# Edge features and times multiplied by their weight matrix per edge, ahead of the scatter, so that the table of edges holds rows of 132 floats

## The chip, the cores and the metric

The kernel runs on one core of one Trainium2 chip. The metric is the time of one execution on the device, in microseconds; it takes 11116.84 us (median of 3 runs, 11109.44 to 11128.29).

## The reference

A graph of N = 12,500 nodes with 64 features and E = 200,000 edges (`src`, `dst`) goes through two networks, with a layer normalisation after each. The first network has three layers that gather the neighbours' rows and sum them per source node; its weights are 64x64. The second network, which the change is about, also uses three arrays of 200,000 x 64 floats, the edge features `ef`, the source times `stf` and the edge times `et`:

```python
target_vec = concat([node_feature[node_j], ef, et], axis=1)      # N_edges x 192
neighbor_emb = target_vec @ W1.T + b1                             # 192 -> 64
neighbors_sum = relu(segment_sum(neighbor_emb, node_i, N))
source_node_vec = segment_sum(concat([node_feature[node_i], stf]), node_i, N) / max(cnt, 1)
out = concat([neighbors_sum, source_node_vec], axis=1) @ W2.T + b2
```

Each edge counts in both directions, and each node has one edge to itself (no features, times of the first edge). The product with W1 is linear, so it can be taken per edge or after the sum over a node's edges.

## The kernel before, in words

All matrix work is in tiles of 128 nodes (T = 98 tiles). Edges are put in order by pairs of tiles: K = 4 places for edges make a chunk, 128 chunks a block, and there are NB = 544 blocks. The stages, in order:

1. **Clear and rank.** SyncE clears the table `by_src` in DRAM, (544 + 1) x 512 rows of ROW floats, by 34 transfers and a few small ones (lines 403 to 408). Beside it a histogram of tile pairs is counted. Then comes ranking, 313 steps of 5 columns of 128 edges: VectorE makes one-hots and masks (`rank`, line 1299), TensorE adds them up and looks the running counts up, five "lanes" per step (`rank`, line 708: three matmul calls per lane, lines 716, 719 and 721), ScalarE copies the running counts out of PSUM before every lane (`snap`, line 972), and VectorE picks out the place of each edge (`select`, line 1290), which goes to `pos`.
2. **Moves.** 2 x 68 `moves` work out which chunk goes where for the gathers: VectorE compares (line 1329), TensorE multiplies with one moving column (line 736, 8 products, 16 passes).
3. **Scatter, beside 1 and 2 and beyond.** SyncE loads batches of PB = 11 columns of edges into one of three slots of `prow`: `ef`, `et`, `stf` (line 418), the three numbers of `meta` (line 419) and the places `ppos` (line 422). GpSimd writes each column to the table by one indirect DMA of 128 rows (line 580, 1562 of them, and one short one at line 593), after the clear is done. SyncE waits on `s_pout` (line 414) before it fills a slot again. VectorE waits for the last scatter at line 1354 and then makes the node array.
4. **wide_by_dst.** Per block, 544 times: GpSimd gathers 128 chunks of 4 rows of the table (line 613); TensorE transposes one-hots (line 747), sums the features by tile with fp32 matmuls (`feature_sum`, line 759: 4 products, 8 passes, the moving operand has FEAT = 193 columns) and picks node rows (line 752); VectorE adds FEAT columns to `node` (line 1414); `rows` has 8 slots.
5. **wide_by_src, then three layers of the first network,** each with a spread (DRAM bound writes of `gathered`) and a sums stage (`sums`, line 825): groups of 4 blocks, in each GpSimd's 4 gathers (line 650), 16 bf16 matmuls (line 836), VectorE's reduction, one-hots and adds, and beside them one block of the features summed by source: SyncE fetches a block of the table to `frows` (2 slots, line 517), TensorE runs `feature_sum` on it, and VectorE adds FEAT columns (line 1479). There are four such stages.
6. **The last layer** (`last`, lines 870 and 1605) takes the sums `facc` of features, times and count and multiplies by W1 and W2.

Every engine runs its own list in order; semaphores order them. Nothing is planned by a program.

## Time and profile before

| | us |
|---|---|
| median of 3 runs | 11116.84 |
| profiled execution, its own time | 11130.16 |
| span of its trace | 11128.4 |
| TensorE busy | 6864.9 (62%) |
| VectorE busy | 6383.6 (57%) |
| GpSimd busy | 5207.2 (47%) |
| ScalarE busy | 3581.3 (32%) |
| moved by DMA | 2320.61 MB, mean 209 GB/s |

The profiled execution is 13 us above the median. A share of busy time is an average over stages that have different limits; the stages are told apart by their windows in the rows below. The granted TensorE clock is printed from 0 to 1, where 1.0 is 2.4 GHz and 0.5 is 1.2 GHz. In a windows row the start and end and the length are followed by busy time and (count) of TensorE's matmuls (PE), its weight loads (PEld), VectorE (DVE), ScalarE (ACT) and GpSimd (POOL), then the granted clock, the DMA share and GB/s. SP is SyncE; a q behind an engine's name is its sequencer.

### The profile page before, as it was taken

Reading aid. Unit: us, or ns where it says so; the run is one execution under the profiler, and the core shown is the slowest. Engines: PE = TensorE matmul, PEld = TensorE weight load, DVE = VectorE, ACT = ScalarE, POOL = GpSimd, SP = SyncE. Lnnn points to the kernel's source line nnn. Section 1 sums busy time; section 2 is a strip of 40 time slices with the busy share of each in tenths; the row PEclk is TensorE's granted clock in tenths of the full one; section 3 lists DMA queues with packets and bytes.
Section 4 is the critical chain, followed back from the end, with each engine's and each line's share of the span. In section 5 each row is a group of like instructions: output and inputs, shape, how many; then the busy total and the mean of one; then the engine's idle time right before and its main releaser. Section 6 shows DMA issues by size and latency. Waiting matters only on the chain.

```text
span 11128.4 us, 191621 instructions
## 1 busy us (share of the span) xinstructions
PE 6864.9 (62%) x46640; PEld 6050.2 (54%) x46640; DVE 6383.6 (57%) x15194; ACT 3581.3 (32%) x10119; POOL 5207.2 (47%) x4833
## 2 busy tenths in 40 slices
PE   7899977800039999556465664556635566656665
PEld 6688867800028888444345554455534455445555
DVE  8899972300036666444575555755567555665556
ACT  0233320000027777333392113921129411481111
POOL 0068887866644444666005661056610366206650
PEclk9999999999999999777697776977769887897776
DMA  9965555555569989556396663966629766896670
GB/s 384 388 179 144 144 144 124 123 142 139 139 176 304 302 297 294 164 166 162 91 396 216 192 188 100 393 220 191 188 51 354 270 191 192 262 361 194 192 172 12
DMA packets 1567388, 2320.61 MB, mean 209 GB/s; under 512 B 974516, under 2 KB 1046056, under 8 KB 1567320
## 3 DMA queue, kind: packets, MB, share of 16 engines
q1 hardware_dynamic: 1227608, 1356.73, 36.5%
q0 software_dynamic: 292608, 911.36, 29.7%
q10 hardware_dynamic: 47104, 51.75, 1.9%
q8 instruction: 26, 0.43, 0.0%
q14 instruction: 42, 0.34, 0.0%
HBM read 1328.55 MB, written 986.78 MB: 208 GB/s over the span
## 4 chain that ended last, share of the span: by engine, by line
issue 28%; PE 22%; DVE 19%; another core or an unknown queue 9%; DMA 9%; ACT 7%; DVEq 5%; ACTq 1%; POOL 1%; SPq 0%; POOLq 0%
PE ps L759 8%; DMA gathered<-ring 5%; PE ps L736 4%; DVE mask L1309 3%; PE ps L836 3%; ACT ring L1074 2%; DVEq L371 2%; ACT hring L1084 2%; PE ps L752 2%; DVE node L1500 2%; DMA frows<-by_src 2%; DVE ohj L1227 1%; DVE oh_s L1368 1%; DVE prod L1293 1%
## 5 line engine op out<-in xcount | busy, mean ns | idle before, releaser
L650 POOL DMA_INDIRECT ring<-gathered,gidx x2176 | 2170.3, 997 | 3328.7 <-DMA gathered<-ring 2118.5
L580 POOL DMA_INDIRECT by_src<-prow,ppos x1562 | 1958.2, 1254 | 1228.5 <-DMA ppos<-pos 707.2
L1382 DVE TENSOR_REDUCE red<-ps 128x256 f32<-128x768 f32 x680 | 650.0, 956 | 1645.5 <-remote 1227.7
L1462 DVE CAST ring<-ps 128x384 bf16<-128x384 f32 x2176 | 1087.5, 552 | 367.7 <-PE ps L752 346.6
L752 PE MATMUL ps<-hring,oht_g 128*128 128x192 bf16 x8704 | 872.4, 246 | 614.9 <-DVE ring L1462 204.7
L836 PE MATMUL ps<-ring,oht_g 128*128 128x192 bf16 x8704 | 1075.5, 286 | 174.7 <-issue 117.5
L759 PE MATMUL ps<-frows,oh_s 128*128 128x193 f32 x2176 | 658.4, 470 | 837.2 <-issue 565.5
L1074 ACT CAST ring<-ps 128x384 bf16<-128x384 f32 x2176 | 1124.5, 519 | 10.6 <-PE ps L752 10.4
L836 PEld LDWEIGHTS ps<-ring,oht_g 128*128 128x128 bf16 x8704 | 954.7, 127 | 291.3 <-issue 251.6
L752 PEld LDWEIGHTS ps<-hring,oht_g 128*128 128x128 fp8e4 x8704 | 659.0, 97 | 828.3 <-issue 786.1
L719 PE MATMUL ps<-snap,oht_e 98*128 98x98 f32 x3130 | 1056.4, 441 | 0.0
L759 PEld LDWEIGHTS ps<-frows,oh_s 128*128 128x128 f32 x2176 | 547.4, 278 | 887.8 <-issue 860.0
L1084 ACT COPY hring<-node 128x192 bf16 x2176 | 853.0, 393 | 55.3 <-issue 46.2
L759 PE MATMUL ps<-rows,ohf 128*128 128x193 f32 x4352 | 848.7, 338 | 26.1 <-ACT ohf L999 19.9
L747 PE MATMUL ps<-ident_bf,oh 128*128 128x128 bf16 x2176 | 211.2, 220 | 1054.2 <-DVE oh L1368 1054.1
L613 POOL DMA_INDIRECT rows<-by_src,gidx x544 | 518.9, 954 | 728.9 <-PE ps L759 265.8
L719 PEld LDWEIGHTS ps<-snap,oht_e 98*128 98x128 f32 x3130 | 819.9, 322 | 0.0
L972 ACT COPY snap<-ps 98x98 f32<-98x98 f32 x1565 | 379.4, 242 | 1182.8 <-PE ps L716 748.5
L747 PEld LDWEIGHTS ps<-ident_bf,oh 128*128 128x128 bf16 x2176 | 167.7, 114 | 1054.8 <-issue 1054.5
L759 PE MATMUL ps<-frows,hring 128*128 128x193 f32 x2176 | 514.9, 390 | 361.0 <-issue 255.1
L759 PEld LDWEIGHTS ps<-rows,ohf 128*128 128x128 f32 x4352 | 700.1, 191 | 43.6 <-ACT ohf L999 30.9
L634 POOL DMA_INDIRECT ring<-gathered,gidx x544 | 558.1, 1026 | 331.2 <-issue 153.4
(226 smaller groups left out, 12892.2 us busy)
## 6 DMA issues: line engine op xcount, KB each, us to landing
gathered<-ring SPq DMA_DIRECT2D x544, 768.0 KB
by_src<-zeros SPq DMA_DIRECT2D x34, 6272.0 KB, 46.3
frows<-by_src SPq DMA_DIRECT2D x544, 392.0 KB
oht_g<-oht SPq DMA_DIRECT2D x544, 256.0 KB, 6.2
gathered<-got SPq DMA_DIRECT2D x136, 776.0 KB
prow<-in_edge_attr_n SPq DMA_DIRECT2D x284, 352.0 KB
bc<-tidrow ACTq DMA_DIRECT2D x313, 160.0 KB
prow<-in_edge_attr SPq DMA_DIRECT2D x142, 352.0 KB
```

The source lines that it names most:

```text
L580: pool.indirect_dma_start(out=table, out_offset=bass.IndirectOffsetOnAxis(ap=ppos[:, s, j:j + 1], axis=0), in_=prow[:, s, j, :], in_offset ...
L613: pool.indirect_dma_start(out=rows[:, c % 8, :, :].rearrange("p k w -> p (k w)"), out_offset=None, in_=table_chunks, in_offset=offsets(g, ...
L634: pool.indirect_dma_start(out=ring1[:, c, :], out_offset=None, in_=gb1, in_offset=offsets(g, c % 4)).then_inc(q.got[g], 16)
L650: pool.indirect_dma_start(out=ring[:, c, :], out_offset=None, in_=gb, in_offset=offsets(g, c % 4)).then_inc(q.got[g], 16)
L719: pe.matmul(where, oht_e[0:T, v, l * P:(l + 1) * P], snap[0:T, (u * LANES + l) % 2, :], start=True, stop=False, skip_group_check=True).the ...
L752: mm = pe.matmul(ps[:, bank + k // 2, k % 2 * HW:(k % 2 + 1) * HW], eight(one_hots)[:, k * P:(k + 1) * P], parts, start=True, stop=True, s ...
L759: mm = pe.matmul(ps[:, bank, 0:FEAT], one_hots[:, k, :], rows_of[:, k, 0:FEAT], start=k == 0, stop=k == K - 1)
L836: mm = pe.matmul(ps[:, 2 * u + e // 2, e % 2 * 256:e % 2 * 256 + HW], ohq[:, c % 8, :, k], ring[:, c, k * HW:(k + 1) * HW], start=k == 0, ...
L1074: act.copy(ring[:, c, 0:2 * HW], ps[:, 2 * (c % 4), 0:2 * HW]).then_inc(q.g, 1)
L1084: act.copy(hring[:, e, :], parts_at(at[e])).then_inc(q.hc, 1)
L1382: return dve.tensor_reduce(red[:, u, :, 0:D], four_of(bank)[:, :, 0:HW].rearrange("p e (a d) -> p e d a", d=D), AX.X, ALU.add)
L1462: dve.tensor_copy(ring[:, c, 2 * HW:4 * HW], ps[:, 2 * (c % 4) + 1, 0:2 * HW]).then_inc(q.gv, 1)
```

## The change

The edge features and edge times of each column (128 edges x 128 floats) are transposed on TensorE and multiplied there by the two matching parts of W1 (`w_z`, 128 x 64), and the product z (64 floats per edge) takes the place of both in the row to be scattered. A row is then z, `stf`, and four small numbers: ROW goes from 196 to 132 floats, FEAT from 193 to 129. The table, its clear, the gathers of stage 4 and the fetches of `frows` shrink with it.

A unit is three columns: 3 transposes (`raw_turned`), one ScalarE copy out of PSUM (`raw_kept`, 128 x 384 fp32), 3 fp32 products with 64 columns (`z_product`), one ScalarE copy into `prow` (`z_kept`, 128 x 192). There are 521 units: 312 stand in the rank steps, one in each (the transposes behind lane 0, the products of the unit before behind lane 2, the ScalarE copies at lanes 2 and 4), 204 in the moves, 6 beside every 4 moves, and 5 behind them. A batch is now 6 columns (two units); a batch's row needs five transfers as before (two into `praw`, three into `prow` and `ppos`). `z_kept` waits until the slot's scatter is done; the scatter waits for `s_z` as well. TensorE waits for all the weights before ranking, and for `s_z` and `s_sel` between ranking and moves. In the last layer the identity stands in the matrix for z, and the self edge's times take the place of the feature sums.

```diff
-PB = 11
-PBATCHES = COLS // PB
-EF, ET, STF, ONE, LS, LD, ROW = 0, D, 2 * D, 3 * D, 3 * D + 1, 3 * D + 2, 3 * D + 4
+ZF, STF, ONE, LS, LD, ROW = 0, D, 2 * D, 2 * D + 1, 2 * D + 2, 2 * D + 4
 FEAT = ONE + 1
+PB = 6
+UC = 3
+UNITS_R = STEPS // 6 * 6
+UNITS_M = 6
...
+PTURNS = (UNITS_R + 2 * (NG // 4) * UNITS_M) // 6
+UNITS = 6 * PTURNS + 5
...
+            def raw(s, use, cols, first=False):
+                if not first:
+                    sp.wait_ge(s_rawt, 6 * use + (2 * s - 4))
+                    sp.nop(nofuse=True)
+                for f, c in ((ef, 0), (et, D)):
+                    v = f[0:P * COLS].rearrange("(c p) d -> p c d", p=P)
+                    sp.dma_start(praw[:, s, 0:cols, c:c + D], v[:, bass.ds((3 * use + s) * PB, cols), :]).then_inc(s_raw[s], 16)
+            def row(s, use, cols, first=False):
                 if not first:
                     sp.wait_ge(s_pout[s], use * (PB * 16))
-                sp.nop(nofuse=True)
-                cols = bass.ds((3 * use + s) * PB, PB)
-                for f, c in ((ef, EF), (et, ET), (stf, STF)):
-                    v = f[0:P * COLS].rearrange("(c p) d -> p c d", p=P)
-                    sp.dma_start(prow[:, s, :, c:c + D], v[:, cols, :]).then_inc(s_plod[s], 16)
-                sp.dma_start(prow[:, s, :, ONE:ROW], meta[:, cols, :]).then_inc(s_plod[s], 16)
-            def places(s, use):
-                sp.dma_start(ppos[:, s, :], pos[:, bass.ds((3 * use + s) * PB, PB)]).then_inc(s_plod[s], 16)
-            AHEAD = -(-3 * PB // LANES)
-            sp.wait_ge(s_meta, 1)
+                    sp.nop(nofuse=True)
+                at = bass.ds((3 * use + s) * PB, cols)
+                v = stf[0:P * COLS].rearrange("(c p) d -> p c d", p=P)
+                sp.dma_start(prow[:, s, 0:cols, STF:STF + D], v[:, at, :]).then_inc(s_plod[s], 16)
+                sp.dma_start(prow[:, s, 0:cols, ONE:ROW], meta[:, at, :]).then_inc(s_plod[s], 16)
+                sp.dma_start(ppos[:, s, 0:cols], pos[:, at]).then_inc(s_plod[s], 16)
...
+            RANKED = STEPS // 4
+            sp.wait_ge(s_tids, 2)
             for s in range(3):
-                load(s, 0, True)
-            sp.wait_ge(s_pos, AHEAD)
+                raw(s, 0, PB, True)
+            sp.wait_ge(s_pos, 4)
             for s in range(3):
-                places(s, 0)
-            with sp.Fori(1, STEPS // AHEAD) as i:
+                row(s, 0, PB, True)
+                raw(s, 1, PB)
+            with sp.Fori(1, RANKED) as i:
                 for s in range(3):
-                    load(s, i)
                     if s == 0:
-                        sp.wait_ge(s_pos, i * AHEAD + AHEAD)
+                        sp.wait_ge(s_pos, 4 * i + 4)
                         sp.nop(nofuse=True)
-                    places(s, i)
+                    row(s, i, PB)
+                    raw(s, i + 1, PB)
...
-                pool.wait_ge(s_plod[s], use * 80 + 80)
+                pool.wait_ge(s_plod[s], use * 48 + 48)
+                pool.wait_ge(s_z, 6 * use + (2 * s + 2))
...
+            def raw_turned(n, v, bank, s, use, first=False):
+                u, h = v % 2, v % 2
+                pe.wait_ge(s_raw[s], 32 * use + 32)
+                if not first:
+                    pe.wait_ge(s_rawc, n - 1)
+                for j in range(UC):
+                    mm = pe.transpose(ps[:, bank + u, j * P:(j + 1) * P], praw[:, s, UC * h + j, :], ident[:, :])
+                mm.then_inc(s_rawt, 1)
+            def z_product(n, v, bank, first=False):
+                u = v % 2
+                pe.wait_ge(s_rawc, n + 1)
+                if not first:
+                    pe.wait_ge(s_z, n - 1)
+                for j in range(UC):
+                    mm = pe.matmul(ps[:, bank + 2 + u, j * D:(j + 1) * D], rawT[:, u, j * P:(j + 1) * P], w_z[:, :],
+                                   start=True, stop=True)
+                mm.then_inc(s_zmm, 1)
...
+                    if l == LANES - 1:
+                        mm.then_inc(s_t, 1)
+                    if l == 0 and m is not None:
+                        raw_turned(n, u, 4, u // 2, m, begin and u < 2)
+                    if l == 2 and not (begin and u == 0):
+                        z_product(n - 1, u + 5, 4, begin and u < 3)
...
+            pe.wait_ge(s_z, UNITS_R)
+            pe.wait_ge(s_sel, STEPS)
...
+                def turn(m, first):
+                    use = UNITS_R // 6 + (k - 1) * (NG // 4)
+                    for v in range(6):
+                        n = 6 * m + (6 * use + v)
+                        if v in (0, 2, 3, 5):
+                            moves(4 * m + (0, 0, 1, 2, 0, 3)[v], (0, 0, 1, 0, 0, 1)[v])
+                        raw_turned(n, v, 0, v // 2, m + use)
+                        if not first or v > 0:
+                            z_product(n - 1, v + 5, 0)
...
+            act.dma_start(w_z[:, :], W1t[D:3 * D, :]).then_inc(s_wload, 16)
+            act.dma_start(w_n1[0:D, :], W1t[0:D, :]).then_inc(s_wload, 16)
+            act.dma_start(w_n1[D:P, :], W1t[2 * D:3 * D, :]).then_inc(s_wload, 16)
...
+            def raw_kept(n, v, bank, first=False):
+                u = v % 2
+                act.wait_ge(s_rawt, n + 1)
+                if not first:
+                    act.wait_ge(s_zmm, n - 1)
+                act.copy(rawT[:, u, :], ps[:, bank + u, 0:UC * P]).then_inc(s_rawc, 1)
+            def z_kept(n, v, bank, s, use, first=False):
+                u, h = v % 2, v % 2
+                act.wait_ge(s_zmm, n + 1)
+                if not first and h == 0:
+                    act.wait_ge(s_pout[s], use * (PB * 16))
+                act.copy(prow[:, s, UC * h:UC * h + UC, ZF:ZF + D],
+                         ps[:, bank + 2 + u, 0:UC * D].rearrange("p (c d) -> p c d", d=D)).then_inc(s_z, 1)
...
+                    if l == 2 and m is not None:
+                        raw_kept(n, u, 4, turn == 0 and u < 2)
+                    if l == 4 and u > 0:
+                        z_kept(n - 1, u - 1, 4, (u - 1) // 2, m, turn == 0)
+                    elif l == 4 and turn > 0:
+                        z_kept(n - 1, 5, 4, 2, UNITS_R // 6 - 1 if m is None else m - 1, turn == 1)
...
+            dve.tensor_copy(w_n2[0:D, 0:D], ident[0:D, 0:D])
...
-                    dve.tensor_scalar(cat[:, :, D:P], facc[:, ts, EF:EF + D], 1.0, None, ALU.mult).then_inc(q.cat, 1)
+                    dve.tensor_copy(cat[:, :, D:P], unit_t).then_inc(q.cat, 1)
...
-                    dve.tensor_tensor(cat2[:, :, 0:D], facc[:, ts, ET:ET + D], unit_t, ALU.add)
+                    dve.tensor_scalar(cat2[:, :, 0:D], facc[:, ts, ZF:ZF + D], 1.0, None, ALU.mult)
```

## Rows read from the trace of the kernel before

**Rows 1.** Windows by stage: stretch, length, busy us (instructions) per engine, clock, DMA, GB/s.

```profile
14.00:630.00 616.00, 514.53 (x2939) 424.73 (x2937) 537.19 (x1367) 81.54 (x332) 0.00 (x0) 1.00 1.00 379
630.00:1610.00 980.00, 929.59 (x4973) 801.92 (x4972) 940.03 (x2469) 299.12 (x1234) 823.16 (x502) 1.00 0.58 143
1610.00:2195.00 585.00, 458.11 (x2144) 457.70 (x2144) 167.94 (x141) 0.00 (x0) 459.65 (x359) 1.00 0.50 123
2195.00:3190.00 995.00, 0.00 (x0) 0.00 (x0) 0.00 (x0) 0.00 (x0) 676.28 (x703) 1.00 0.56 140
3270.00:4450.00 1180.00, 1078.68 (x8541) 999.81 (x8539) 734.43 (x2670) 873.08 (x2263) 502.39 (x528) 1.00 0.92 299
5883.00:6712.00 829.00, 509.93 (x3136) 465.88 (x3136) 463.10 (x1040) 98.82 (x263) 530.53 (x536) 0.77 0.68 188
7276.00:8120.00 844.00, 511.92 (x3184) 466.96 (x3184) 471.23 (x1054) 100.39 (x265) 537.56 (x543) 0.78 0.67 188
8739.00:9590.00 851.00, 513.95 (x3184) 467.49 (x3185) 471.34 (x1055) 100.39 (x265) 553.87 (x544) 0.78 0.68 188
9975.00:10850.00 875.00, 535.02 (x3271) 488.03 (x3271) 486.66 (x1095) 102.66 (x269) 537.84 (x544) 0.77 0.68 185
```

**Rows 2.** The clears: their issue (first and last start), size and landing; first scatter.

```profile
L408 SPq DMA_DIRECT2D by_src<-zeros x34: 782/16608/24364, 14.4 to 561.4; - x34
...
by_src<-zeros SPq DMA_DIRECT2D x34, 6272.0 KB, 46.3
...
634.07 1.14 POOL L580 DMA_INDIRECT by_src<-prow,ppos  x1 [632.53 <-DMA ppos<-pos]
```

**Rows 3.** Groups of instructions in ranking, 640 to 1600 us: busy us, mean ns.

```profile
L719 PE MATMUL ps<-snap,oht_e 98*128 98x98 f32 x2448 | 826.1, 441 | 0.0
L580 POOL DMA_INDIRECT by_src<-prow,ppos x490 | 811.7, 1656 | 149.4 <-issue 149.4
```

**Rows 4.** Groups of instructions in the moves, 1745 to 2195 us.

```profile
L736 PE MATMUL ps<-steps,cmp 99*128 x2080 | 443.9, 352 | 3.2 <-DVE cmp L1329 3.2
...
L580 POOL DMA_INDIRECT by_src<-prow,ppos x266 | 368.6, 1386 | 91.3 <-issue 80.8 <-DMA ppos<-pos 10.5
```

**Rows 5.** One rank step in order of time, VectorE and GpSimd: start, us, instruction.

```profile
999.97 0.96 POOL L580 DMA_INDIRECT by_src<-prow,ppos  x1 [0.30 <-issue]
...
1000.14 0.45 DVE L1227 TENSOR_TENSOR ohi<-tid_s,bin_lane 128x490 bf16<-128x490 bf16 x1
...
1001.24 2.32 POOL L580 DMA_INDIRECT by_src<-prow,ppos  x1 [0.30 <-issue]
...
1001.33 1.40 DVE L1309 SCALAR_TENSOR_TENSOR mask<-bc,tid_f,upper_bf 128x128 bf16<-128x128 bf16 x5
...
1002.64 0.70 DVE L1293 TENSOR_TENSOR prod<-ps,ohj 128x490 f32<-128x490 f32 x1
```

**Rows 6.** fp32 transposes and products of a layer, in order of time.

```profile
5397.03 1.75 PE L853 MATMUL ps<-ident,ring 128*128 128x128 f32 x7 [8.14 <-DVE ring L1558]
5398.58 3.19 PE L859 MATMUL ps<-wts,ring 128*128 128x128 f32 x14
```

**Rows 7.** Feature matmuls in wide_by_dst, 3300 to 4450 us: busy us, mean ns.

```profile
L759 PE MATMUL ps<-rows,ohf 128*128 128x193 f32 x4156 | 808.7, 338 | 21.4 <-ACT ohf L999 16.5 <-issue 4.4
```

**Rows 8.** SyncE's register moves, 1745 to 2195 us and 2200 to 3150 us (min/median/max ns).

```profile
L418 SPq MOVE prow<-in_edge_attr_n x50: 5/29/29, 1745.0 to 2194.9; - x50
...
L418 SPq MOVE prow<-in_edge_attr_n x120: 1/698/1421, 2208.4 to 3140.3; - x120
```

**Rows 9.** Chain that ended last, by line: wide_by_dst, first and last sums stage.

```profile
by line: PE ps L759 40.6%; PE ps L752 10.1%; issue 8.8%; another core or an unknown queue 8.4%; ACT ohf L999 8.0%; PE ps L747 7.6%; ACT got L1006 6.6%; DMA rows<-by_src,gidx 4.5%; ACT loc L1016 1.8%; ACT loc L993 1.3%; DVE got L1396 0.3%; A
...
by line: issue 33.1%; another core or an unknown queue 15.5%; PE ps L759 11.4%; PE ps L836 10.1%; DVEq L371 5.6%; DVE node L1500 5.1%; DVE oh_s L1368 4.6%; DVE red L1382 3.9%; DMA frows<-by_src 2.8%; DVEq L1500 2.1%; DVE node L1479 1.7%; DV
...
by line: issue 30.5%; another core or an unknown queue 16.2%; PE ps L759 9.0%; PE ps L836 7.3%; DVEq L371 6.0%; DMA frows<-by_src 5.6%; DVE node L1500 5.3%; DVE red L1382 5.0%; DVE oh_s L1368 4.8%; DVEq L1500 2.8%; DVE node L1479 1.6%; DVE 
```

**Rows 10.** Size of the fetches of the table in the sums stages.

```profile
frows<-by_src SPq DMA_DIRECT2D x544, 392.0 KB
```

135 lines of the change are left out of this document (81 added, 54 removed).

## The prediction

> **What bounds the kernel now.** I read the windows by stage first. Clear, ranking, moves and scatter take the first 3190 us; then come wide_by_dst (3270 to 4450) and four sums stages of 829 to 875 us, 3399 us together [rows 1]. In the first 3190 us the last thing to end is the scatter: it starts at 634 us, because its semaphore of the clears comes last (34 transfers of 6272 KB, the last one issued at 561.4 and landing some 46 us later, near 608), and GpSimd then issues 1563 indirect DMAs [rows 2]. From 14 to 630 us the DMA share is 1.00, so the clear is bandwidth. Behind it GpSimd sets the time, at three paces: 490 scatters in 960 us of ranking, 1.96 us each [rows 3]; 266 in 450 us of moves, 1.69 us [rows 4]; 703 in the last 995 us, 1.42 us, in which TensorE, VectorE and ScalarE do nothing [rows 1].
>
> Why three paces: a scatter takes 0.96 us and the next starts 0.30 later, 1.27 us in all, unless it starts while VectorE runs the run from the first one-hot to the last mask (1000.14 to 1002.64, 2.5 us). The one that started at 1001.24 took 2.32 us and ended 0.9 us after that run; the one at 999.97 took 0.96 [rows 5]. So a step of T us has room for 1 + floor((T - 2.5) / 1.27) scatters: 2 at the present 3.92 us (960 us over 2448/10 steps), as the 490 in 960 us show, and 3 from 5.04 us on. In the moves each of the 130 compares costs a scatter (450 - 10.5 - 266 x 1.27) / 130 = 0.79 us [rows 4].
>
> **The clear.** ROW goes to 132/196 = 0.673 of its size, so the 594 us of clears become 400 us and end near 414 instead of 608. But ranking now waits for the first `praw`, which is queued on SyncE behind the clears, and cannot start before they have landed: I put it at 418; now it starts near 1600 - 313 x 3.92 = 373. Four steps and the loads of a batch later the scatter starts, near 450, 184 us earlier than now.
>
> **Ranking.** TensorE is busy 929.59 us in 980 [rows 1], 3.7 us per step. A unit adds three fp32 transposes and six fp32 passes. Seven transposes take 1.55 us before the products start, 0.22 each [rows 6]; a pass with a single moving column takes 443.9 / 2080 = 0.213 us in the moves [rows 4], so 64 columns cost about that too. Unit: 3 x 0.22 + 6 x 0.213 = 1.94 us. The bounds of one transpose or pass are 0.13 us (808.7 / 4156 = 0.195 for 193 columns, scaled to 128 [rows 7]) and 0.34 us (826.1 / 2448, the look-ups [rows 3]): 1.2 to 3.0 us per unit. I take 1.94, since the moves stand right behind ranking. A step then lasts 5.65 us, bound by TensorE: VectorE needs 3.92, and GpSimd needs 5.04 for the three columns that a step now supplies. 313 steps are 1768 us, ending near 2186 (now: 1600). ScalarE's two copies fit into its idle time (299 us busy of 980); the one that waits for `s_pout` stands ahead of the next `snap`, and behind that all of ranking would wait, but with GpSimd at 5.04 against 5.65 it seldom does.
>
> **Moves.** 34 turns of 18 columns. TensorE: 6 x 1.94 + 4 x 3.42 (16 passes) = 25.3 us. GpSimd: 18 x 1.27 + 4 x 0.79 = 26.0 us. With both so near each other I take 27 us: 918 us. I add 20 us for the lag of the scatter behind the units, 17 for the last 15 columns' own path and 20 for a slow start of the moves. The scatter ends near 3161, against 3190: 29 us gained, of the 184 that the clear gives. The rest goes because the last 995 us at 1.42 us a column are replaced by ranking at 5.65/3 = 1.88. Should a unit cost 1.2 us, GpSimd's 5.04 is the step and ranking is 190 us shorter; at 3.0 us it is 330 us longer. These are the ends for this part: gain 220, loss 300.
>
> SyncE issues five transfers per batch as before, but a batch is 6 columns. In the moves its register instructions take 29 ns, and in the idle tail 698 ns [rows 8]; a batch of 11 columns then took 995 x 11 / 703 = 15.6 us. I cost it at nothing, since TensorE and VectorE now work until the end of the scatter; what it costs without that cover is the second rival.
>
> **wide_by_dst.** Its chain goes for 40.6% of 1150 us, 467 us, through the feature matmuls, and for 4.5% through the gathers of the table [rows 9]. Both shrink by a third with FEAT and ROW: 156 + 17. Against that, ScalarE is busy 873 of 1180 us and VectorE 734 [rows 1] with waits on registers besides, so something of it is taken over: I take 140, bounds 40 and 230 (the DMA share of 0.92 falls as well, which may free more).
>
> **Sums stages.** The feature matmuls hold 11.4% of the chain in the first and 9.0% in the last, the `frows` fetches 2.8% and 5.6% [rows 9]: 347 and 143 us over the 3399. The fetch goes from 392 KB [rows 10] to 264. A third of both is 163 us. GpSimd's floor is 544 x 1.27 = 691 us per stage, below the 829 to 875, so it does not stop this; VectorE's own order and its tile reads do in part. I take 110, bounds 0 and 200. The node array is narrower too (its memset ahead of wide_by_dst): 5 us. The last layer exchanges operations one for one: nothing.
>
> **Sum.** 29 + 5 + 140 + 110 = 284 us off the profiled execution's 11130 us (span 11128.4 plus 1.8): 10,846. The median of the runs is 13 us lower, so 10,830 us.
>
> **Rivals.**
> (1) Ranking is bound by GpSimd, not TensorE: a step of about 5.1 us. For it: the feature matmuls do 193 columns in 0.195 us, so a pass with 64 might be short [rows 7]; against it: the 0.213 us passes right beside. It gives 313 x 0.55 = 172 us more: 10,660 us. The Trainium skill ("TensorE: Matmul & The Clock Gate", section "LDWEIGHTS (loading the stationary operand)") says that a weight load takes its columns divided by 1.2 in ns, 107 ns for 128; by that nine loads make a unit of 0.96 us, an estimate from the page, and this rival would hold. The moves' passes, with 128 loaded columns and one moving one, take twice that, so the trace disagrees there.
> (2) Slower: SyncE ticks at 0.70 us an instruction during the moves. Its price: 3 batches x 15.6 = 46.7 us a turn instead of 27, 670 us if it holds for all 34 turns: 11,500 us. It decides from 284 / 19.7 = 14 turns on. For it: ticks are there in the whole idle tail, and batches are smaller; against it: none in the moves now [rows 8].
> (3) Ranking steps of 6.6 us, because ScalarE's waits and the hand-overs between units add up on TensorE: 313 x 0.95 = 297 us more: 11,125 us, no change.
> (4) The set-up as forecast, but wide_by_dst and sums hardly shrink, since the matmuls' wait was beside VectorE's: 50 us in all instead of 250: 11,030 us.
>
> **How the numbers follow.** Forecast 0.50, (1) 0.12, (2) 0.12, (3) 0.12, (4) 0.14. What can be told from no change is 0.2%, 22 us. Faster: 0.50 + 0.12 + 0.14 and half of (3), 0.82; same 0.03; slower: (2) and the rest of (3), 0.15. The forecast's own range is 10,700 to 10,980 (set-up +-110, the stages +-90). To hold eight in ten I reach to most of (1) and to (3): 10,600 to 11,120; (2) stays out.
>
> **What would show it.** Clears ending near 414 us. A rank step of 5.65 us with TensorE over 95% busy and exactly three scatters in it; ranking ending near 2190 and the scatter near 3160. SyncE's MOVE at 29 ns in the moves. wide_by_dst near 1040 us in place of 1180 and sums stages of 800 to 850 us. I am wrong if a step is under 5.2 or above 6.2 us, if TensorE stands still while ScalarE waits for `s_pout`, or if SyncE sets the moves' pace.

## The result: 2.3% slower here, slower on one other chip and faster on two

| us | before | changed | ratio, 95% interval |
|---|---|---|---|
| first comparison | 11114.13 | 11369.81 | 1.0228 [1.0211, 1.0246] |
| chip B (e5) | 10514.22 | 10351.78 | 0.9846 [0.9827, 0.9866] |
| chip C (e10) | 10516.83 | 10339.04 | 0.9828 [0.9811, 0.9844] |
| chip D (e16) | 11064.04 | 11224.12 | 1.0148 [1.0119, 1.0178] |

The changed kernel was forecast at 10,830 us, faster; in the comparison that counts it took 11,370 and was slower. Every median is of executions in the faster of two states; one execution of e5 (10,789 us) and one of e14 (10,545 us) fell in the slower one and are left out.

The experiments ran on other chips: A (e1 to e4, e13, e14), B (e5 to e8), C (e9 to e12), D (e15, e16) and E (e17, e18). The kernel before takes 10,510 to 10,530 us on A, B and C, and 11,060 to 11,070 on D and E. The chip of the first comparison is of the second kind, called stalling below, since its traces show what A, B and C do not: SyncE's register instructions that last about 0.7 us, and hand-overs from TensorE to the next engine that come about 0.7 us late or more, with nothing in the profile that holds them. The changed kernel itself ran on the first chip and on B, C and D; on A and E only edited versions of it ran.

The profile of the changed kernel, first comparison. Windows by stage (columns as in [rows 1]): ranking, moves and end of scatter, wide_by_dst, the first sums stage.

```profile
440.00:2470.00 2030.00, 1755.89 (x8870) 1586.86 (x8869) 1208.31 (x3059) 551.76 (x2141) 1024.07 (x924) 0.50 0.43 102
2500.00:3480.00 980.00, 847.74 (x4010) 832.44 (x4009) 166.46 (x141) 159.35 (x415) 639.74 (x614) 0.50 0.45 105
3560.00:4670.00 1110.00, 914.84 (x8317) 828.11 (x8316) 676.68 (x2601) 841.84 (x2210) 494.02 (x520) 0.97 0.79 250
6160.00:6960.00 800.00, 458.14 (x3064) 412.91 (x3064) 448.77 (x1024) 96.76 (x257) 514.25 (x519) 0.75 0.63 169
```

The same kernel on chip C:

```profile
440.00:2140.00 1700.00, 1690.00 (x8875) 1597.70 (x8875) 1207.52 (x3058) 552.01 (x2142) 1050.82 (x924) 1.00 0.51 121
2160.00:3000.00 840.00, 838.11 (x4033) 837.92 (x4032) 167.58 (x141) 165.16 (x415) 628.88 (x612) 1.00 0.53 123
3080.00:4080.00 1000.00, 891.97 (x8527) 821.34 (x8528) 704.46 (x2664) 870.36 (x2265) 520.12 (x534) 1.00 0.91 284
5480.00:6200.00 720.00, 441.12 (x3113) 397.27 (x3113) 456.54 (x1039) 106.28 (x260) 552.90 (x529) 0.80 0.70 190
```

The same 8870 or so products of ranking take 2030 us on one chip and 1700 on the other; TensorE stands still for 274 us of the one and 10 of the other.

The granted clock differs in these rows too, 0.50 against 1.00 in ranking, and a reader will suspect it. It is not the cause. Of the four executions of the changed kernel in the first comparison two have a mean clock of 0.71 and two of 0.87, at 11,375 and 11,360 us against 11,365 and 11,382; on D they are 11,223.25 (0.716) and 11,225.0 (0.870). The look-up product (L769) takes 442 ns on average in ranking in the first comparison and 441 ns on C.

Where the time went, from the first and last instructions of each stage (us; the kernel before and the changed one, first comparison, then chip C; each difference is changed less before):

| | before | changed | difference | before, C | changed, C | difference |
|---|---|---|---|---|---|---|
| scatter starts | 634.1 | 443.8 | -190 | 632.4 | 441.7 | -191 |
| ranking ends | 1598.5 | 2485.5 | +887 | 1598.3 | 2150.3 | +552 |
| last scatter starts | 3188.5 | 3495.8 | +307 | 3068.6 | 3017.8 | -51 |
| from there to the first gather | 50.1 | 47.3 | -3 | 50.1 | 47.4 | -3 |
| first gather to last feature sum, wide_by_dst | 1210.6 | 1167.2 | -43 | 1132.2 | 1031.6 | -101 |
| four sums stages, gather to last feature sum | 3457.9 | 3445.6 | -12 | 3108.1 | 3095.3 | -13 |

All of the loss lies in the ranking and the moves; the stages behind them gained, though less than forecast. The clears gave their 190 us on both chips.

How ranking is slower shows in the waits from 700 to 2100 us (engine, line, what it waited for, us in total, times, longest). First comparison, then chip C:

```profile
ACT snap L1060 <- PE ps L766: 639.3, 653, 2.8
...
ACT snap L1060 <- PE ps L769: 193.4, 113, 3.5
PEld ps L766 <- issue: 181.6, 162, 1.9
```

```profile
ACT snap L1060 <- PE ps L766: 902.2, 977, 1.7
...
PEld ps L766 <- ACT snap L1060: 37.0, 126, 0.5
ACT snap L1060 <- PE ps L769: 20.1, 29, 0.7
```

On chip C ScalarE waits nearly always for TensorE's update (L766), which is what it looks like when TensorE binds. In the first comparison TensorE waits too, for "issue" (nothing that the profile shows) and for snapshots that came late. One such place, in the same position of the program on both (start, duration, engine and line, idle before). First comparison:

```profile
1011.97 1.48 PE L752 MATMUL ps<-w_z,rawT 128*128 128x64 f32 x6
...
1013.24 0.30 PE L766 MATMUL ps<-ohj,ohi 128*98 128x98 bf16 x1
1013.25 1.72 POOL L599 DMA_INDIRECT by_src<-prow,ppos  x1 [0.30 <-issue]
...
1015.09 0.00 SPq L437 DMA_DIRECT2D prow<-in_edge_attr_n  x1
...
1015.14 0.24 ACT L1060 COPY snap<-ps 98x98 f32<-98x98 f32 x1 [3.30 <-remote]
```

Chip C:

```profile
1011.30 0.30 PE L766 MATMUL ps<-ohj,ohi 128*98 128x98 bf16 x1
...
1011.38 1.72 POOL L599 DMA_INDIRECT by_src<-prow,ppos  x1 [0.31 <-issue]
...
1011.55 0.67 SPq L438 DMA_DIRECT2D prow<-meta  x1
1011.64 0.24 ACT L1060 COPY snap<-ps 98x98 f32<-98x98 f32 x1 [1.73 <-PE ps L766]
```

The update of the running counts (L766) ends at 1013.54, and the snapshot that needs nothing else starts at 1015.14, 1.6 us later, with SyncE's late transfer beside it; on chip C it starts 0.04 us after.

What comes late there is not ScalarE. The trace records each semaphore's updates, and the one that this snapshot waits for is recorded at 1015.12, 1.6 us behind the end of the product; ScalarE starts 0.02 us later. Nothing on ScalarE is in the way. So it is with 244 of the 249 late snapshots counted below: each starts within 0.11 us (median 0.023) of a recorded update of its semaphore, and none has an update in time. On chip C the update is recorded 14 ns behind the end of the product (median; 15 at the 90th percentile). The updates of ScalarE's and VectorE's own instructions in ranking stand 9 to 13 ns behind their ends on both chips. VectorE, which also waits for TensorE (L771), waits up to 3.6 us in the first comparison and 0.9 on C. The ends of matmuls are modelled in the profile, so the trace does not tell whether TensorE finished late or only its update was late.

I counted this over all updates from 700 to 2100 us in the instruction records (of the kernel before, 700 to 1500): **late** is a snapshot that starts over 0.6 us after the end of its update.

| kernel | chip | late | step, us |
|---|---|---|---|
| before | first | 0 of 1018 | 3.93 |
| changed | first | 249 of 1048 | 6.68 |
| changed (e16) | D | 228 of 1097 | 6.38 |
| changed (e5, e10) | B, C | 0 of 1258, 0 of 1260 | 5.56 |
| one scatter of six (e15) | D | 0 of 1260 | 5.56 |
| VectorE filled (e17) | E | 55 of 1190 | 5.88 |
| copy moved (e18) | E | 19 of 1220 | 5.74 |

The step here is the length of the window divided by a fifth of its snapshots. In the expectations below steps are from the first histogram to the last snapshot over 313, about 0.2 us more (5.79 for 5.56, 6.86 for 6.68; for e16 it is 6.59, for e17 6.14, for e18 6.00). In the first comparison all 249 late ones are among the 633 updates that end while a scatter runs or within 0.4 us behind it, and none among the 415 at which GpSimd is idle. On SyncE the same chip shows such delays in the kernel before, in the idle tail [rows 8]. In the same tail on chip C (e9) the register moves take (min/median/max ns)

```profile
L418 SPq MOVE prow<-in_edge_attr_n x118: 29/29/29, 2208.2 to 3015.4; - x118
```

and over the whole trace 429 (before) and 315 (changed) register instructions of SyncE last 0.6 to 0.8 us in the first comparison, 118 to 269 on D and E, none on A, B and C.

### The profile page after: what moved, and what is told of

The parts are those of the page before. It is cut to its first block, busy times and chain, and to the rows that moved or that the text cites. A ratio compares the mean times of both kernels' runs of the same rounds, so it can differ in the third digit from the quotient of the medians.

```text
span 11372.8 us, 207012 instructions
## 1 busy us (share of the span) xinstructions
PE 7579.3 (67%) x51329; PEld 6739.7 (59%) x51329; DVE 6336.6 (56%) x15195; ACT 3914.9 (34%) x11161; POOL 4901.5 (43%) x4833
## 4 chain that ended last, share of the span: by engine, by line
PE 37%; issue 21%; another core or an unknown queue 10%; DVE 8%; ACT 8%; DMA 7%; SPq 4%; DVEq 3%; ACTq 1%; POOL 1%; POOLq 0%
PE ps L769 7%; PE ps L831 6%; PE ps L752 5%; PE ps L908 5%; DMA gathered<-ring 4%; SPq L420 3%; PE ps L794 3%; PE ps L743 3%; PE ps L766 2%; ACT ring L1189 2%; ACT hring L1199 2%; DVEq L384 2%; PE ps L824 1%; ACT ohf L1114 1%
## 5 line engine op out<-in xcount | busy, mean ns | idle before, releaser
L599 POOL DMA_INDIRECT by_src<-prow,ppos x1563 | 1689.1, 1081 | 1806.1 <-ACT prow L1051 949.7
L908 PE MATMUL ps<-ring,oht_g 128*128 128x192 bf16 x8704 | 1195.7, 303 | 305.3 <-issue 245.0
L908 PEld LDWEIGHTS ps<-ring,oht_g 128*128 128x128 bf16 x8704 | 1027.9, 132 | 397.4 <-issue 344.9
L831 PE MATMUL ps<-frows,oh_s 128*128 128x129 f32 x2176 | 499.4, 402 | 939.8 <-issue 666.5
L1189 ACT CAST ring<-ps 128x384 bf16<-128x384 f32 x2176 | 1115.9, 514 | 10.9 <-PE ps L824 10.6
L769 PE MATMUL ps<-snap,oht_e 98*128 98x98 f32 x3130 | 1060.3, 442 | 0.0
L831 PEld LDWEIGHTS ps<-frows,oh_s 128*128 128x128 f32 x2176 | 432.3, 295 | 1009.4 <-issue 819.1
L752 PE MATMUL ps<-w_z,rawT 128*128 128x64 f32 x3126 | 755.6, 415 | 123.2 <-ACT rawT L1044 106.4
L769 PEld LDWEIGHTS ps<-snap,oht_e 98*128 98x128 f32 x3130 | 830.4, 326 | 0.0
L752 PEld LDWEIGHTS ps<-w_z,rawT 128*128 128x128 f32 x3126 | 729.3, 333 | 143.1 <-ACT rawT L1044 115.2
L1211 ACT CAST hring<-oh_s 128x512 f32<-128x512 bf16 x272 | 177.0, 651 | 1801.7 <-DVE oh_s L1483 1617.3
L661 POOL DMA_INDIRECT ring<-gathered,gidx x544 | 554.8, 1020 | 332.2 <-issue 153.4
L831 PE MATMUL ps<-rows,ohf 128*128 128x129 f32 x4352 | 649.0, 294 | 61.9 <-ACT ohf L1114 45.3
L766 PE MATMUL ps<-ohj,ohi 128*98 128x98 bf16 x1565 | 497.9, 318 | 282.9 <-issue 185.0
```

What stands on the lines that cost most here:

```text
L599: pool.indirect_dma_start(out=table, out_offset=bass.IndirectOffsetOnAxis(ap=ppos[0:lanes, s, j:j + 1], axis=0), in_=prow[0:lanes, s, j, : ...
L752: mm = pe.matmul(ps[:, bank + 2 + u, j * D:(j + 1) * D], rawT[:, u, j * P:(j + 1) * P], w_z[:, :], start=True, stop=True)
L766: pe.matmul(ps[0:T, 0, 0:T], ohi[:, v, :, l], ohj[:, v, :, l], start=False, stop=False, skip_group_check=True).then_inc(s_upd, 1)
L769: pe.matmul(where, oht_e[0:T, v, l * P:(l + 1) * P], snap[0:T, (u * LANES + l) % 2, :], start=True, stop=False, skip_group_check=True).the ...
L831: mm = pe.matmul(ps[:, bank, 0:FEAT], one_hots[:, k, :], rows_of[:, k, 0:FEAT], start=k == 0, stop=k == K - 1)
L908: mm = pe.matmul(ps[:, 2 * u + e // 2, e % 2 * 256:e % 2 * 256 + HW], ohq[:, c % 8, :, k], ring[:, c, k * HW:(k + 1) * HW], start=k == 0, ...
```

## Experiments

Theory A: GpSimd's scatters make the hand-overs between TensorE and ScalarE late. Theory B: the unit's own copies, in ScalarE's order ahead of the snapshots, hold the step.

**e1, chip A.** Five of six scatters left out, and the waits that count them changed to match (only the main lines of each edit are shown here and below).

```diff
-                for j in range(PB):
-                    to_table(s, j, P)
+                to_table(s, 0, P)
```

> The changed kernel with only the first of the six scatters of each batch issued (five of six edges never reach the table, so the features that are summed are those of one edge in six; everything else, the units of transposes and products too, stays). Theory A (GpSimd's back-to-back scatters slow the hand-overs between TensorE and ScalarE): with GpSimd nearly idle the ranking step falls from 6.60 us to its TensorE work of 5.7 us, ranking ends near 2205 us instead of 2486, the moves take their 27 us per turn, and the whole is near 11,000 us. Theory B (the unit's own copies on ScalarE, in order ahead of the snapshots, hold the step): the step stays at 6.5 to 6.6 us, ranking ends at 2450 to 2490 us and the whole is at 11,330 to 11,370 us.

10325.06 us, 0.9805 [0.9789, 0.9821] of before (10530.4), ranking ends at 2149.5. It looked like theory A.

**e2, chip A.** Both copies of a unit cut to 8 elements.

```diff
-                act.copy(rawT[:, u, :], ps[:, bank + u, 0:UC * P]).then_inc(s_rawc, 1)
+                act.copy(rawT[:, u, 0:8], ps[:, bank + u, 0:8]).then_inc(s_rawc, 1)
...
-                act.copy(prow[:, s, UC * h:UC * h + UC, ZF:ZF + D],
-                         ps[:, bank + 2 + u, 0:UC * D].rearrange("p (c d) -> p c d", d=D)).then_inc(s_z, 1)
+                act.copy(prow[:, s, UC * h, ZF:ZF + 8], ps[:, bank + 2 + u, 0:8]).then_inc(s_z, 1)
```

> The changed kernel with the unit's two ScalarE copies cut to 8 elements each (the products and the table's edge part then hold mostly zeros); every wait, transpose, product and scatter stays. Theory B: ScalarE gets back 0.4 us of 483 ns and 0.2 us of 323 ns per ranking step, the snapshots come in time, the step is 5.8 us, ranking ends near 2240 us and the whole is near 11,120 us. Theory A: the hand-overs stay slow, the step is 6.4 to 6.6 us, ranking ends at 2430 to 2490 us and the whole is at 11,310 to 11,370 us.

10350.32 us, 0.9826 [0.9809, 0.9842] of before, ranking ends at 2152.1. It looked like theory B as well. Two cures that exclude each other had both worked in full, and the kernel before took 5% less on this chip than in the first comparison: the changed kernel itself had to be run on such a chip.

**e5, chip B.** The changed kernel itself.

> The changed kernel unchanged, to stand on the same chip as the experiments. If the chip of the first four experiments is merely quicker everywhere, its ranking step here is near 5.6 us too and the cut copies and the scatters left out explained nothing; if both did something, the step is 6.5 to 6.9 us here as well and the whole is 1.5 to 2.5% over the kernel before.

10351.78 us, ranking ends at 2151.2. So e1 and e2 had changed nothing that matters on such a chip, and the change is 1.5% faster here.

**e6 and e7, chip B.** One of the two copies cut at a time.

> The changed kernel with only the copy of the products (323 ns, behind the last snapshot of a step) cut to 8 elements; the copy of the transposes stays whole. Theory B, sharpened: this copy stands ahead of the snapshot that TensorE needs first in the next step, with only a lookup and a mask product of TensorE beside it; if it is the cause, the step falls to 5.5 to 5.6 us. Theory A (scatters slow hand-overs) or the copy of the transposes as the cause: the step stays at 6.5 us or more.

> The changed kernel with only the copy of the transposes (483 ns, behind the third snapshot) cut to 8 elements; the copy of the products stays whole. It has 1.3 us of products beside it on TensorE; if the copy of the products is the cause the step stays at 6.5 us or more, and if this one is it falls to 5.5 to 5.6 us. Theory A: 6.3 us or more.

10358.81 and 10359.66 us, both steps as in e5: misses. On a chip without stalls neither copy costs anything. On a stalling chip neither was cut.

**e3, chip A.** Rows of 132 floats without the units.

```diff
+                sp.dma_start(prow[:, s, 0:cols, ZF:ZF + D], ve[:, at, :]).then_inc(s_plod[s], 16)
...
-                        raw_turned(n, u, 4, u // 2, m, begin and u < 2)
...
-                        z_product(n - 1, u + 5, 4, begin and u < 3)
```

> The changed kernel without its units: rows of 132 floats whose first 64 are loaded from the edge features, no transposes, no products, no copies of them (the edge times and the product with the matrix are left out). What narrow rows alone give. If GpSimd keeps the 2554 us that it takes for the scatter in the kernel before, it starts near 445 us and ends near 3000 us; with the later stages as in the changed kernel the whole is near 10,870 us. If, with no ranking beside its first part any more ahead of it, GpSimd is slower or faster by the masks that hold it, the end moves between 2950 and 3150 us. Later stages: same as in the changed kernel to 10 us in both theories.

10265.71 us, 0.9754 [0.9737, 0.977]; the last scatter starts at 2931.7, a little ahead of the 2950 to 3150 that I allowed. Against 3017.8 for the changed kernel on chip C the units and their loads cost 86 us of scatter end. I read this as TensorE binding to the end with them (840 us of moves at 838 busy on C), and GpSimd without them. (My 10,870 stood on the first chip's 11,114, a ratio of 0.978.)

**e4, chip A.** The kernel before with the feature products and additions cut to 129 columns.

```diff
-                    mm = pe.matmul(ps[:, bank, 0:FEAT], one_hots[:, k, :], rows_of[:, k, 0:FEAT], start=k == 0,
+                    mm = pe.matmul(ps[:, bank, 0:129], one_hots[:, k, :], rows_of[:, k, 64:193], start=k == 0,
```

> The kernel before with the products of the feature sums and VectorE's additions cut from 193 to 129 columns; rows of 196 floats are still cleared, scattered, gathered and loaded (64 of the 193 summed columns are left out). If the shorter products and additions gave the 44 us in the first feature sums and the 12 us in the others, the whole is near 11,060 us; if the narrower gathers gave them, the time stays at 11,114 us. My forecast's terms for the same edit were 140 and 110 us, that is 10,865 us.

10467.33 us against 10530.4: -63 us, 0.9939 [0.9923, 0.9956]. wide_by_dst takes 1077.8 us, between the 1132.2 of e9 and the 1031.6 of e10 (chip C): 54 us by the shorter products and additions, 46 by what else the change brings (the narrower gathers among it; not tested singly). The four sums stages show nothing from the shorter products (3114 us against 3108).

**e9, e10, chip C.** Both kernels, to have their traces on one chip.

> The kernel before, unchanged, to have its trace on the same chip as the experiments. On the chips of the experiments so far it took 10,530 and 10,514 us, and not the 11,114 us of the first comparison, and none of their traces has a register instruction of SyncE near 0.70 us, where the first comparison's two have 429 and 315. If these stalls are what made the first comparison slow, this trace has none wherever the whole is near 10,520 us, the clears end and the ranking ends as at first (608 and 1600 us), the scatter ends near 3070 us instead of 3188, the first feature sums take 1080 to 1120 us instead of 1211 and each of the others 770 to 790 us instead of 865. If the chip is one of the slow kind, the stalls are back and the whole is near 11,100 us.

> The changed kernel, unchanged, once more beside the kernel before. Without stalls of 0.70 us in the trace: ranking step 5.8 us, TensorE without a pause through the ranking, 1.2 to 1.9% faster than before. With them: ranking step 6.9 us and 1.8 to 2.8% slower than before.

10511.93 and 10339.04 us (the columns "C" above), as expected but for wide_by_dst of the kernel before, 1132 us where I had 1080 to 1120. The ranking of the kernel before ends at the same time on both kinds of chip, 1598.3 and 1598.5. In its first sums stage (5620 to 6350 us) the largest wait on chip C is that of ScalarE for the gathers to land:

```profile
ACT gidx L988 <- DMA ring<-gathered,gidx: 567.9, 128, 6.8
```

**e11, chip C.** ScalarE's cast of the one-hots in wide_by_dst halved.

```diff
-                    act.copy(ohf[:, c % 2], oh[:, c % 4].rearrange("p n k -> p k n")).then_inc(q.ohf, 1)
+                    act.copy(ohf[:, c % 2, 0:2, :], oh[:, c % 4].rearrange("p n k -> p k n")[:, 0:2, :]).then_inc(q.ohf, 1)
```

> The changed kernel with ScalarE's cast of the one-hots for the first feature sums cut from 512 to 256 columns (675 ns, once for each of 544 blocks); TensorE uses the two halves that are there twice, so all its instructions stay, and half of the edges are summed into wrong rows. If ScalarE is what bounds this stage (four copies of 2.0 us in all for a block of 1.96 us), the stage falls from about 1017 us to 870 to 930 us, where TensorE's 0.90 of the time binds it. If TensorE's feature product bounds it, as my forecast took it, it falls by less than 20 us.

TensorE uses the two quarters that are there twice, so that all its products stay. The stage takes 994.5 us for 1031.6, where I expected a fall of 90 us or more if ScalarE bounds it, and under 20 if TensorE does. Changed kernel (3080 to 4080), then e11 (3080 to 4040), by line:

```profile
L831 PEld LDWEIGHTS ps<-rows,ohf 128*128 128x128 f32 x4264 | 516.8, 191 | 142.2 <-ACT ohf L1114 133.6 <-issue 0.3
L1114 ACT CAST ohf<-oh 128x512 f32<-128x512 bf16 x534 | 359.6, 673 | 0.0
```

```profile
L831 PEld LDWEIGHTS ps<-rows,ohf 128*128 128x128 f32 x4248 | 514.2, 191 | 116.4 <-ACT ohf L1114 112.3 <-issue 0.3
...
L1114 ACT CAST ohf<-oh 128x256 f32<-128x256 bf16 x531 | 231.1, 435 | 0.0
```

and e11's window:

```profile
3080.00:4040.00 960.00, 881.24 (x8495) 814.24 (x8494) 705.60 (x2655) 759.09 (x2255) 522.61 (x531) 1.00 0.92 294
```

Some 128 us less on ScalarE bring 37. Behind ScalarE's casts comes TensorE, 0.92 busy now and 0.89 before, but not alone. The chain that ended last, by line, in the changed kernel (3080 to 4080) and in e11 (3080 to 4040):

```profile
by line: DMA rows<-by_src,gidx 24.1%; PE ps L831 23.5%; issue 12.7%; ACT ohf L1114 10.6%; ACT got L1121 6.3%; PE ps L824 6.0%; PE ps L819 4.0%; DVEq L384 3.5%; ACT loc L1131 2.0%; ACT loc L1108 1.6%; POOL rows L640 1.1%; DVE got L1511 0.8%;
```

```profile
by line: DMA rows<-by_src,gidx 36.6%; PE ps L831 30.0%; PE ps L824 8.4%; issue 8.0%; PE ps L819 5.3%; DVEq L384 2.9%; ACT ohf L1114 2.2%; POOL rows L640 1.4%; DVE got L1511 1.2%; DVE hring L1520 0.6%; DVE got L1510 0.4%; ACT loc L1108 0.4%;
```

With the cast halved its part falls from 10.6% to 2.2%, and the landing of the gathers rises from 24.1% to 36.6%, at a DMA share of 0.92. On this chip the stage has three bounds close together: gathers, feature products, casts.

**e8, chip B.** The copy of the products behind the first snapshot of the next step.

```diff
-                    if l == 4 and u > 0:
-                        z_kept(n - 1, u - 1, 4, (u - 1) // 2, m, turn == 0)
+                    if l == 0 and u > 1:
+                        z_kept(n - 2, u - 2, 4, (u - 2) // 2, m, turn == 0)
```

> The changed kernel with the copy of the products moved from behind the last snapshot of a step to behind the first snapshot of the next, where TensorE has the three transposes of 0.22 us each beside it; nothing is left out. Theory B, sharpened: the step is 5.5 to 5.7 us, the scatter ends 250 to 350 us earlier than in the changed kernel, and the whole is 2.0 to 3.0% under the changed kernel, 1 to 2% under the kernel before. Theory A: no change, within 0.5% of the changed kernel.

10329.52 us, 0.9817 [0.9801, 0.9834]: 22 us under the changed kernel, a tenth of what I expected. Ranking ends 7 us earlier.

**e12, chip C.** The same, and the cast of the places moved to VectorE.

> The changed kernel with the copy of the products behind the first snapshot of the next step, and in the first feature sums the cast of the places (four columns, 208 ns for each block) moved from ScalarE to VectorE; nothing is left out. If ScalarE bounds that stage, it falls by 40 to 110 us and the whole is 0.6 to 1.3% under the changed kernel; if TensorE or the gathers bound it, it stays within 0.3% of it.

10331.74 us against 10339.04; wide_by_dst takes 1010.6 us for 1031.6, a fall of 21 us where I expected 40 to 110, and of both parts 7 us are left in the whole, within the spread of the runs.

**e13 and e14, chip A.** An idle copy of 644 ns ahead of the copy of the products, at its old and at its new place.

```diff
+                if bank == 4:
+                    act.copy(scr[:, u, :, :], ps[:, bank + 2 + u, 0:UC * D].unsqueeze(1).to_broadcast([P, 3, UC * D]))
```

> The changed kernel with an idle copy of 128x576 elements into a buffer that nobody reads, in front of each copy of the products during ranking, behind the last snapshot of a step: about 0.65 us more on ScalarE once per step, the size of one stall of the first chip. On a chip without stalls: TensorE has only a lookup and a mask product of about 0.5 us beside snapshot and copies there, so nearly all of the hold reaches the step: 5.8 us becomes 6.3 to 6.5 us, ranking ends 160 to 210 us later, the whole is near 10,520 us. If instead such a hold is hidden, the step stays at 5.8 to 5.9 us, and stalls of this kind at this place can't be what made the first chip's step long.

> The same hold of about 0.65 us, but with the copy of the products and the hold behind the first snapshot of the next step, where TensorE has 1.14 us of lookup, mask product and transposes beside it. If the place decides, the step stays at 5.75 to 5.9 us, ranking ends within 30 us of 2146 us and the whole is within 30 us of 10,330 us; if any hold on ScalarE costs its length, the step is 6.3 to 6.5 us here too.

10371.82 and 10339.33 us; ranking ends at 2180.4 and 2143.1. The hold costs 29 us at the old place where I expected 160 to 210, and nothing at the new one. One hold per step at one place is not what the first chip had; a quarter of all hand-overs late is.

**e15 and e16, chip D**, of the stalling kind: e1's kernel and the changed one.

> The changed kernel with only the first of the six scatters of each batch (five of six edges never reach the table). On a chip with stalls of 0.70 us (the kernel before near 11,110 us): with the scatters gone in ranking, late hand-overs drop to under a fifth and the step falls from 6.9 us to 5.8 to 6.0 us, if the scatters bring the stalls; it stays at 6.8 us if they come from elsewhere. On a chip without them (before near 10,520 us): 5.8 us, as before.

> The changed kernel, unchanged, beside it. With stalls: step 6.9 us and 1.8 to 2.8% slower than before; without: 5.8 us and 1.3 to 1.9% faster.

e16 is 1.48% slower than before, under the 1.8 to 2.8% that I expected with stalls, and e15 2.15% faster (10822.86 us, 0.9785 [0.9757, 0.9814]; two executions of each). The window from 700 to 2100 us of e16 and of e15, then the waits in it of e16 and of e15 (its line numbers are two less):

```profile
700.00:2100.00 1400.00, 1261.93 (x6363) 1138.34 (x6363) 869.06 (x2196) 396.97 (x1536) 725.70 (x658) 0.50 0.44 105
```

```profile
700.00:2100.00 1400.00, 1391.30 (x7303) 1315.37 (x7303) 996.90 (x2518) 456.23 (x1764) 123.24 (x126) 1.00 0.43 90
```

```profile
ACT snap L1060 <- PE ps L766: 679.5, 685, 3.2
...
ACT snap L1060 <- PE ps L769: 243.9, 143, 3.4
...
PEld ps L766 <- issue: 150.4, 181, 1.9
```

```profile
ACT snap L1058 <- PE ps L764: 895.7, 966, 1.7
...
PEld ps L764 <- ACT snap L1058: 36.1, 126, 0.5
ACT snap L1058 <- PE ps L767: 29.0, 42, 0.7
```

This shows theory A on this chip: late hand-overs in ranking need the scatters. With five of six gone goes every late one; ranking ends at 2150.2, as on A, B and C, instead of 2401.6, and TensorE is 0.99 busy instead of 0.90. The granted clock of these two rows differs, but both executions of e15 take 10,823 us, at a mean clock of 0.864 and of 0.723. The edit takes away the issuing on GpSimd and the writes to the table together, so it does not tell which of them it is. Nor does it rule out that the place of the unit's copies matters as well; e18 bears on that. The later stages, whose gathers stayed, keep this chip's length (the four sums stages 3409 us, e16's 3411, chip C's 3095). SyncE's slow register instructions go with the scatters too: all 118 of e15 lie behind 4210 us, where e16 has 139 before 3450 us.

**e17, chip E**, of the stalling kind. Four more masks per step on VectorE into an unused buffer.

```diff
+                for l in range(4):
+                    dve.scalar_tensor_tensor(scr[:, u, l, :], bc[:, u, l * P:(l + 1) * P],
```

> The changed kernel with four more mask operations of 345 ns each per ranking step on VectorE, into a buffer that nobody reads: VectorE goes from 71% to about 95% busy of a 5.6 us step. On a chip with stalls: if a busy VectorE keeps them away, late hand-overs (over 0.6 us) drop to under a third of the changed kernel's 21 to 24%, and the step falls from 6.6 or 6.9 us to 5.8 to 6.2 us, work added and time won; if VectorE has nothing to do with them the step stays at 6.5 us or rises to 7. On a chip without stalls: 5.8 to 6.0 us, no gain.

11077.44 us, 1.0009 [0.9996, 1.0022] of before, with 1.4 us of work added to each step. The changed kernel itself did not run on chip E, so it is compared with e16 on chip D. That E stalls like D shows in the stages that the edit leaves alone: from the end of ranking to the last scatter e17 takes 1020 us, e18 below 1002 and e16 1000, against 868 on C. The kernel before takes 11,067 us on E and 11,064 on D. The window of e17:

```profile
700.00:2100.00 1400.00, 1337.69 (x6907) 1243.55 (x6906) 1175.38 (x3333) 433.25 (x1667) 1182.02 (x716) 1.00 0.49 114
```

and by line, the scatters and the added masks:

```profile
L600 POOL DMA_INDIRECT by_src<-prow,ppos x716 | 1183.0, 1652 | 218.3 <-issue 216.2 <-DMA ppos<-pos 1.5 <-ACT prow L1052 0.6
...
L1426 DVE SCALAR_TENSOR_TENSOR scr<-bc,tid_f,upper_bf 128x128 bf16<-128x128 bf16 x952 | 269.6, 345 | 0.0
```

VectorE goes from 0.62 to 0.84 busy, a scatter from 1104 ns to 1652, late hand-overs from 21% to 5%. This fits the kernel before, which has none in ranking: VectorE is busy 772 of the 800 us from 700 on, and half of the scatters take over 1.3 us there (mean 1.66). That it is this which keeps the late ones away is argued, not shown: one edited kernel, compared across two chips.

**e18, chip E.** e8's kernel on a stalling chip.

> The changed kernel with the copy of the products behind the first snapshot of the next step. On a chip with stalls: the hand-overs are hit as before, so the step stays between 6.3 and 6.9 us and the whole is 1 to 2.5% slower than before. On a chip without: 1.8% faster than before.

11047.76 us, 0.9985 [0.9975, 0.9995] of before: my expectation was wrong, for the better. Only 19 of 1220 snapshots are late and TensorE is 0.99 busy:

```profile
700.00:2100.00 1400.00, 1379.77 (x7078) 1274.20 (x7079) 968.92 (x2441) 442.23 (x1709) 883.57 (x733) 0.50 0.50 117
```

This is the version to keep: level with the kernel before, or 0.15% under it, on a stalling chip, and 1.8% faster on B (e8). Against the changed kernel it stands by way of before, 0.9985 on E to 1.0148 on D. So both edits work on a stalling chip, the scatters left out and the copy moved, and neither theory alone tells the whole. The late hand-overs are not merely covered in e18: there are few of them, with scatters of 1207 ns on average, hardly slower than e16's 1104. Why a copy that costs nothing elsewhere decides so much there is not settled.

## Why the prediction was wrong

The step that failed is **"a step then lasts 5.65 us, bound by TensorE"**, and with it the sentence that ScalarE's two copies fit into its idle time. As a sum it was right: TensorE was busy 1755.9 us over 2030, and where nothing stalls the step is 5.56. I left out that TensorE's binding rests on a chain TensorE, ScalarE, TensorE that passes five times per step, and that this chip delays the hand-over from TensorE while scatters run: 249 of 1048 came over 0.6 us late, and the step is 6.68. It cost 335 us in ranking (2485.5 for 2150.3) and about 140 in moves and the end of the scatter (1010 us for 868). That is 478 us against chip C. Against the forecast it is less, since without stalls the scatter ends near 3018 and I had put it at 3161: it ended 335 us behind the forecast, and the later stages gave about 195 us less than theirs, which makes 530 of the 540 us missed.

The evidence was in the trace: SyncE's 698 ns for a 29 ns move [rows 8]. I took these ticks for a matter of SyncE's in an idle kernel, made a rival of them for the moves, and gave SyncE's transfers the price. They came in ranking, and between TensorE and the engines that wait for it. What the kernel before had in ranking and the changed one has less of is a VectorE that holds scatters up [rows 5]; I used that only to say how many scatters fit into a step. Whether it is what kept the delays away is not shown (e17, e18).

Point by point:

- The clears: scatter starts at 443.8, forecast "near 450". Right.
- The unit at 1.94 us: a step of 5.56 less the 3.7 of before is 1.86. Right, and rival 1 is out. By the Trainium skill ("TensorE: Matmul & The Clock Gate", section "LDWEIGHTS (loading the stationary operand)") the estimate was 0.96 us, and the trace does not agree with that.
- Moves: 918 us and 57 of lags, 975, against 868 on chip C and 1010 in the first comparison. Even without stalls the sum was 107 us too long; 27 us a turn is 25.5 at most (868 over 34).
- Scatter end 29 us earlier: 51 earlier on chip C, 307 later here.
- SyncE at nothing: right for ranking in the first comparison, where GpSimd waits for ScalarE's copy (548 us of the window) and for no load of SyncE's.
- wide_by_dst -140: -101 on chip C, -43 here. The chain's 40.6% in the feature products [rows 9] was no measure of what they free: e4 took 54 us by them, and e11 shows the gathers and ScalarE's casts right beside.
- Sums -110: -12 and -13. That is near the bound "0", and e4 says that the products there bring nothing. On chip C the feature product holds 5.8% of the chain of the first sums stage before (e9) and 2.1% after (e10), where I had read 11.4% on the first chip.
- Rival 3, ranking steps of 6.6 us by ScalarE's waits and hand-overs, had 0.12 and named the step's length and place; 6.68 is what was measured. Its cause, waits and hand-overs that add up by themselves, was not it: e6, e7 and e13 show that they hardly add up where nothing stalls. Rival 4 held at the same time. I had them as exclusive, and priced neither with the other: 11,125 plus the 200 us that rival 4 takes off is 11,325.
- Range: it ended at 11,120 on the slow side and left rival 2 (11,500) out, with the only trace at hand from a chip that had ticks in it.

On chips B and C the forecast's sign holds, and so does its mechanism in ranking, with 162 to 178 us gained for 284. Even there the sum is in part luck: the set-up gave 51 us for 29, and the later stages about 115 for 255.

Open: what makes a chip stall (the same program, the same inputs), what the scatters do there to TensorE's updates, why VectorE's work and the moved copy keep the delays away, and how much of the 5% between the kinds of chip in the later stages is the same thing.

One rival to "the chip" is untested. The stalling traces also lack records: that of the changed kernel holds 91,011 semaphore updates in the first comparison and 91,243 on D, against 169,795 on C, for the same 207,012 instructions. So it may be the recording of the trace that falls behind on these chips and holds the engines up. Against it: the kernel before lacks almost half of its snapshots' updates in ranking there (540 of 1018 are recorded) and has no late one. For it: e15, with no late one in ranking, has 1259 of 1260. Every time on record comes with a recorded clock, so no run tells what the kernels take unrecorded.

## To carry to other kernels

A price that is read from a busy time holds only for the chain that feeds it: where two engines pass work back and forth several times per step, multiply a late hand-over by the number of passes before calling the busier one the bound. A row that is too long for what it does (698 ns for a register move) can turn up between other engines where the change lays them bare; ask what kept it away until now. Where an experiment and its opposite both "cure", run the kernel in question on that chip first; for e17 and e18 on chip E that was not done. A late start is not yet a fault of the engine that starts: look up when its semaphore was updated.

## What was not expected of the hardware

- Two kinds of chip: the kernel before takes 10,510 to 10,530 us on three and 11,060 to 11,120 on three, with the same mean durations of the compute instructions compared in ranking (L769 441 and 442 ns, snapshot 241 ns on both, masks 345 and 344). What differs is the gaps, and by them the sign of a change of 2%.
- On the stalling kind TensorE's semaphore update comes over 0.6 us, mostly 0.7 to 1.7 us, behind the end of its product before 21 to 24% of the changed kernel's snapshots, only while a scatter runs or within 0.4 us behind it, and never in ranking with five of six scatters gone. ScalarE's and VectorE's updates are on time.
- With more work on VectorE such a kernel took 11,077 us against 11,224 without, though on two chips of this kind (before at 11,067 and 11,064), so that the gain is not shown on one chip.
- The granted clock is printed 0.50 through the set-up in some executions and 1.00 in others (e16 and e15 above) with equal durations of the same products (L769 443 ns in e16, 442 in e15 and, on chip C with 1.00 printed, 441) and equal times of the whole. In these kernels it explained no difference there.
